# Windowed attention and a ternary feed-forward layer on one core: the attention stage written anew, with head tiles on TensorE and each even half of the keys kept twice

## What is computed

```python
xn = layernorm(x)
qkv = xn @ Wqkv + bqkv                       # 16 heads of 32 features
scores = q_block @ keys_of_3_blocks.T / sqrt(512)   # blocks of 128 tokens
scores = where(abs(kpos - qpos) <= 128 and 0 <= kpos < S, scores, -1e30)
attn = softmax(scores) @ values_of_3_blocks
a = attn @ Wout + bout
h = xn @ (scale * ternary(w_fc)).T + gate * (xn @ v.T @ fast_b.T @ u.T)
f = max(h, 0)**2 @ (scale * ternary(w_proj)).T
out = x + a + f
```

## Time and profile before

| | before |
|---|---|
| median of 3 runs | 2811.32 us |
| the profiled execution | 2808.96 us |
| its span, first to last instruction | 2807.0 us |
| mean granted TensorE clock | 0.984 |
| busy: TensorE, VectorE, ScalarE, GpSimd | 97%, 72%, 61%, 23% |
| instructions | 61651 |

### The profile page before, as it was taken

How to read it: one execution, slowest core, us unless ns; L and a number is a source line. 1 busy time by engine, 2 the same in 40 slices (tenths; PEclk the granted TensorE clock), 3 DMA queues, 4 the chain that set the end, 5 groups by cost and what they waited for, 6 DMA issues and landing times. The chain is left out here.

```text
span 2807.0 us, 61651 instructions
## 1 busy us (share of the span) xinstructions
PE 2728.3 (97%) x20744; PEld 2397.7 (85%) x20744; DVE 2023.4 (72%) x5704; ACT 1712.8 (61%) x3745; POOL 639.1 (23%) x812
## 2 busy tenths in 40 slices
PE   6999999999999999999999977999999999999998
PEld 5899999999999999999999965888888888888887
DVE  4899999999999999999999966444444444444443
ACT  3678778787787877878778756333333333333332
POOL 3223323233233332323323220111111111111111
PEclk9999999999999999999999987999999999999999
DMA  3333333333333333333333333111111111111101
GB/s 114 92 97 93 99 94 105 89 92 100 95 98 96 94 99 94 99 94 94 99 95 95 97 90 137 49 46 49 45 50 46 49 46 45 46 45 46 45 31 45
DMA packets 177015, 219.98 MB, mean 78 GB/s; under 512 B 32112, under 2 KB 115280, under 8 KB 176192
## 3 DMA queue, kind: packets, MB, share of 16 engines
q1 hardware_dynamic: 175840, 215.31, 26.7%
q0 software_dynamic: 864, 0.73, 0.1%
HBM read 80.91 MB, written 33.55 MB: 41 GB/s over the span
## 5 line engine op out<-in xcount | busy, mean ns | idle before, releaser
L716 ACT ACTIVATE probs<-neg_scores,neg_max 128x384 f32<-128x384 f32 (+1 forms) x1024 | 630.8, 616 | 341.9 <-DVE neg_max L789 335.3
L789 DVE CUSTOM_DVE_ANT_0 neg_scores<-score_ps,mask 128x384 f32<-128x384 f32 (+1 forms) x1024 | 559.9, 547 | 109.0 <-PE score_ps L913 56.2
L1441 ACT ACTIVATE relu<-up_ps,fc_scale 128x512 f32<-128x512 f32 x256 | 176.3, 689 | 656.9 <-PE up_ps L1572 656.9
L800 DVE TENSOR_TENSOR pT_lo<-pT_ps,pT_hi 128x384 f16<-128x384 f32 (+1 forms) x1024 | 561.2, 548 | 13.5 <-ACT xT_hi L729 4.9
L1515 DVE SCALAR_TENSOR_TENSOR sq<-up_ps,relu 128x512 f32<-128x512 f32 x256 | 177.0, 691 | 536.2 <-ACT relu L1441 536.2
L934 PE MATMUL pT_ps<-ident,probs 128*128 128x128 f32 x3040 | 506.6, 275 | 12.4 <-ACT probs L716 9.8
L727 ACT CAST pT_hi<-pT_ps 128x384 f16<-128x384 f32 (+1 forms) x1024 | 470.1, 459 | 3.8 <-PE pT_ps L934 3.5
L913 PE MATMUL score_ps<-stack 96*128 96x128 f32 (+2 forms) x1536 | 448.9, 347 | 0.0
L934 PEld LDWEIGHTS pT_ps<-ident,probs 128*128 128x128 f32 x3040 | 366.0, 141 | 81.3 <-DVE oT_lo L804 12.9
L1582 PE MATMUL down_ps<-proj_T,sq_hi 128*128 128x512 f32 x1024 | 408.9, 399 | 0.3 <-DVE sq_lo L1498 0.2
L1584 PE MATMUL down_ps<-proj_T,sq_lo 128*128 128x512 f32 x1024 | 404.3, 395 | 0.0
(11 more groups left out here) (165 smaller groups left out, 5186.1 us busy)
## 6 DMA issues: line engine op xcount, KB each, us to landing
stack<-qk_parts SPq DMA_DIRECT2D x1536, 64.0 KB, 2.1
x_in<-in_L_attn_x SPq DMA_DIRECT2D x64, 256.0 KB, 3.2
y<-in_L_attn_x SPq DMA_DIRECT2D x64, 256.0 KB, 3.0
partial<-y SPq DMA_DIRECT2D x64, 256.0 KB, 3.4
f_x_in<-in_L_attn_x SPq DMA_DIRECT2D x64, 256.0 KB, 2.7
part_in<-partial SPq DMA_DIRECT2D x64, 256.0 KB, 3.6
out<-f_y SPq DMA_DIRECT2D x64, 256.0 KB, 2.0
fc_in<-in_L_ffn_w_fc SPq DMA_DIRECT2D x16, 256.0 KB, 6.2
```

Of the source, the lines that this page charges most:

```text
L716: nc.scalar.activation(probs[:, r, cols], neg_scores[:, r, cols], ACT.Exp, bias=neg_max[:, s % 4:s % 4 + 1], scale=-1.0).then_inc(probs_do ...
L789: nc.vector.tensor_tensor_reduce(out=neg_scores[:, r, cols], in0=score_ps[:, r, cols], in1=mask[:, cols], scale=-SCORE_SCALE, scalar=3e38, ...
L800: last = nc.vector.tensor_tensor(pT_lo[:, s % 4, cols], pT_ps[:, r, cols], pT_hi[:, s % 4, cols], ALU.subtract)
```

## The change

The feed-forward stage now comes first. It is the same, but for three things: it adds x where it added `partial`, and writes x plus feed-forward to `partial`; it also stores the turned, normalised x, hi and lo, to a new DRAM tensor (8 DMAs of 256 KB per tile); and its 14 inner tiles are a hardware loop of 7 rounds of two tiles, with semaphore values in registers.

The attention stage (`attention_stage`) reads the turned x from DRAM, so its layernorm and transposes of x are gone. It has 128 steps of four heads by two query blocks (one step does what 8 steps did before). In a step t:

- `scores`: for each of the two blocks three passes (q_hi k_hi, q_lo k_hi, q_hi k_lo), each four matmuls, one for each head: 32 rows by 384 columns, at four places of the array (`tile_position=(h * DH, 0)`) and into four PSUM banks. The `stack` tile and its DMAs are gone.
- Keys are kept for six blocks; `copy_keys` on GpSimd copies the new even half to the front, so that 384 keys are always in one piece.
- The exponential also sums its row (`accum_out`), VectorE inverts the sums, GpSimd multiplies the probabilities in SBUF, TensorE turns them, and ScalarE alone copies them to an f32 tile `pT`; no f16 parts.
- `probs_times_values`: values are stationary (128 x 32, plain f32), the turned probabilities are moving, with four heads at four column places (`tile_position=(0, h * DH)`): per step 8 matmuls of 256 columns and 8 of 128. The product is already turned for the output projection.

The cut diff (of 1732 lines):

```diff
@@ feed-forward, loop over tiles
-            for i in range(NT):
-                tile(i, i % 2)
+            tile(0, 0)
+            with eng.Fori(0, (NT - 2) // 2) as pair:
+                for n in range(2):
+                    tile(2 * pair + 1 + n, (1 + n) % 2)
+            tile(NT - 1, (NT - 1) % 2)
@@ feed-forward, sync
+            def store_xT(i, par):
+                for b in range(NB):
+                    sp.wait_ge(xT_done, NB * i + b + 1)
+                    settle(sp, ticks)
+                    for low, xT in enumerate((xT_hi, xT_lo)):
+                        sp.dma_start(xT_rows(xT_dram, NB * i + b, low),
+                                     xT[:, par, :, b * P:(b + 1) * P].bitcast(F32)).then_inc(xT_stored[b], 16)
@@ attention, all of it replaced; GpSimd
+            def normalise(t, b):
+                ...
+                pool.wait_ge(rcp_done, 2 * t + b + 1)
+                for h in range(HC):
+                    u = b * HC + h
+                    nc.gpsimd.tensor_scalar(probs[:, u, cols], probs[:, u, cols], sum_rcp[:, u:u + 1], None, ALU.mult
+                                            ).then_inc(normalised, 1)
+            def copy_keys(u):
+                i, c = where(u)
+                pool.wait_ge(qk_done, u + 1)
+                nc.gpsimd.tensor_copy(k_hi[:, c, 0:2, :], k_hi[:, c, 4:6, :])
+                nc.gpsimd.tensor_copy(k_lo[:, c, 0:2, :], k_lo[:, c, 4:6, :]).then_inc(keys_copied, 1)
@@ ScalarE
+            def exp(t, b, h):
+                ...
+                nc.scalar.activation(probs[:, u, cols], probs[:, u, cols], ACT.Exp, bias=neg_max[:, u:u + 1], scale=-1.0,
+                                     accum_out=prob_sum[:, u:u + 1]).then_inc(exped, 1)
+            def copy_pT(t, b, h):
+                ...
+                act.wait_ge(turned, 8 * t + b * HC + h + 1)
+                if t >= 1:
+                    act.wait_ge(pv_done, t)
+                nc.scalar.copy(pT[:, h, first + seen.start:first + seen.stop, :].rearrange("p w t -> p (w t)"),
+                               pT_ps[:, h % 2, seen.start * P:seen.stop * P]).then_inc(pT_done, 1)
+            for t in range(STEPS + 3):
+                ...
+                for h in range(HC):
+                    if 1 <= t <= STEPS:
+                        copy_pT(t - 1, 1, h)
+                    if t < STEPS:
+                        exp(t, 0, h)
+                if job_a(t) is not None:
+                    qk_high(job_a(t), A_NUMBER[t], a_bank(t))
+                for h in range(HC):
+                    if t < STEPS:
+                        exp(t, 1, h)
+                    if h == 0 and 1 <= t <= STEPS:
+                        oT_high(t - 1)
+                    if t < STEPS:
+                        copy_pT(t, 0, h)
@@ VectorE
+                if t < STEPS:
+                    find_max(t, 0)
+                    invert_sums(t, 0)
+                if job_a(t) is not None:
+                    qk_low(job_a(t), a_bank(t))
+                if t < STEPS:
+                    find_max(t, 1)
+                if 1 <= t <= STEPS:
+                    oT_low(t - 1)
+                if t < STEPS:
+                    invert_sums(t, 1)
@@ TensorE
+                for pass_ in range(PASSES):
+                    q = q_lo if pass_ == 1 else q_hi
+                    keys = k_lo if pass_ == 2 else k_hi
+                    for h in range(HC):
+                        rows = slice(h * DH, (h + 1) * DH)
+                        last = nc.tensor.matmul(score_ps[:, h, cols], q[rows, c, place, :],
+                                                keys[rows, c, first + seen.start:first + seen.stop, :],
+                                                start=(pass_ == 0), stop=(pass_ == PASSES - 1),
+                                                tile_position=(h * DH, 0))
+                ...
+                for n, (blk, places, seen) in enumerate(parts):
+                    for h in range(HC):
+                        ...
+                        last = nc.tensor.matmul(job_ps[strip, bank, places.start * P:places.stop * P],
+                                                values[:, blk % VR, head * DH:(head + 1) * DH], pT[:, h, seen, :],
+                                                start=(n == 0), stop=(n == len(parts) - 1), tile_position=(0, h * DH))
+            for t in range(STEPS + 3):
+                if t < STEPS:
+                    scores(t, 0)
+                for part in range(QUARTERS):
+                    if 1 <= t <= STEPS:
+                        turn_probs(t - 1, 1, part)
+                    run_a(t, part)
+                if t < STEPS:
+                    scores(t, 1)
+                if 1 <= t <= STEPS:
+                    probs_times_values(t - 1)
+                for part in range(QUARTERS):
+                    if t < STEPS:
+                        turn_probs(t, 0, part)
+                    run_b(t, part)
```

More of the change, by code:

```diff
@@ L46, in settle, with xT_rows @@
     eng.sem_inc(ticks[eng.engine], 1)
+    eng.sem_inc(ticks[eng.engine], 1)
 def block_rows(dram, block):
     return dram[bass.ds(block * P, P), :]
+def xT_rows(dram, block, low):
+    return dram[bass.ds((2 * block + low) * P, P), :].rearrange("p (k t) -> p k t", k=DC)
 def identity_on_pool(pool, nc, ident, zeroed, ready):
@@ L1270, in _, with feed_forward_stage @@
                 nc.scalar.copy(low_out[:, n * D:(n + 1) * D], turn_ps[0:3 * DH, n, :]).then_inc(u_copied, 1)
-def feed_forward(nc, x, partial, fast_b, w_fc, w_proj, u, v, gate, out):
+def feed_forward_stage(nc, x, fast_b, w_fc, w_proj, u, v, gate, xT_dram, partial):
     F = w_fc.shape[0]
@@ L1334, in feed_forward @@
         stored = [sem(f"stored{b}") for b in range(NB)]
+        xT_stored = [sem(f"xT_stored{b}") for b in range(NB)]
         block = ctx.enter_context(nc.Block())
@@ L1367, in _ @@
                 sp.sem_inc(stored[b], 16)
+            def store_xT(i, par):
[5 more added lines that the diff above has]
+                                     xT[:, par, :, b * P:(b + 1) * P].bitcast(F32)).then_inc(xT_stored[b], 16)
+            store_xT(0, 0)
             def tile(i, par):
@@ L1375, in tile @@
                         settle(sp, ticks)
-                        sp.dma_start(block_rows(out, NB * (i - 1) + b), y[:, b, :]).then_inc(stored[b], 16)
+                        sp.dma_start(block_rows(partial, NB * (i - 1) + b), y[:, b, :]).then_inc(stored[b], 16)
                 for b in range(NB):
-                    sp.dma_start(part_in[:, b, :], block_rows(partial, NB * i + b)).then_inc(part_here[b], 16)
+                    sp.dma_start(part_in[:, b, :], block_rows(x, NB * i + b)).then_inc(part_here[b], 16)
+                if not is_last(i):
+                    store_xT(i + 1, 1 - par)
             tiles(sp, tile)
@@ L1382, in _ @@
                 sp.wait_ge(y_done, NB * (NT - 1) + b + 1)
-                sp.dma_start(block_rows(out, NB * (NT - 1) + b), y[:, b, :]).then_inc(stored[b], 16)
+                sp.dma_start(block_rows(partial, NB * (NT - 1) + b), y[:, b, :]).then_inc(stored[b], 16)
             for b in range(NB):
                 sp.wait_ge(stored[b], 16 * (NT + 1))
+                sp.wait_ge(xT_stored[b], 32 * NT)
         @block.gpsimd
@@ L1415, in xT_high @@
                 act.wait_ge(x_turned, NB * i + b + 1)
+                wait(act, xT_stored[b], 32 * (i - 1))
                 nc.scalar.copy(xT_hi[:, par, :, b * P:(b + 1) * P],
@@ L1610, with attention, feed_forward @@
+HELD = {}
+def attention(nc, x, Wqkv, bqkv, Wout, bout, partial):
+    HELD["attention"] = (Wqkv, bqkv, Wout, bout)
+def feed_forward(nc, x, partial, fast_b, w_fc, w_proj, u, v, gate, out):
+    xT_dram = nc.dram_tensor("xT", [2 * x.shape[0], x.shape[1]], F32, kind="Internal").ap()
+    feed_forward_stage(nc, x, fast_b, w_fc, w_proj, u, v, gate, xT_dram, partial)
+    attention_stage(nc, *HELD["attention"], xT_dram, partial, out)
 _INS = ["L0_attn_x", "L0_attn_Wqkv", "L0_attn_bqkv", "L0_attn_Wout", "L0_attn_bout", "L0_ffn_fast_b", "L0_ffn_w_fc",
```

1257 lines of the change are left out of this document (464 added, 793 removed).

## The result

The changed kernel takes 2876.74 us, the median of 4 runs (2875.95 to 2878.27), against 2811.33 us (2810.37 to 2813.68, 4 runs): the ratio is 1.0232, with a 95% interval of 1.0214 to 1.025. The forecast was 2765 us, faster; the time lies within its range of 2650 to 3000, but on the other side of no change. The profiled execution took 2878.27 us, with a span of 2875.8.

What follows compares the result with a forecast made beforehand. TensorE was taken to bound the kernel, at 12.09 us per attention step against 12.54. The span was 2807.0 - 128 x 0.45 + 14 = 2763, with 2 us around it 2765 us; range 2650 to 3000.

Steps and rivals of the forecast that it cites:

- The chain: Attention: cross-engine waits from turning probabilities to turning them a step later, 11.2 us; as rival it binds, 2651 us, 17%.
- Hidden by TensorE's work: Attention step: the 11.2 us of waits around the engines lie below TensorE's 12.09 us, so they cost nothing.
- TensorE's sum: Attention step: TensorE's own work adds up to 12.09 us, 0.45 less than the 12.54 of before.
- Values: TensorE's product of probabilities with values, plain f32: two heads at a time, 2.58 us a step.
- Scores: TensorE's 24 score matmuls of a step: six passes of four heads at 0.22 us, 1.32 us.
- Turns and changes of work: TensorE per step: 24 transposes 1.92 us, plus 0.6 for changes between kinds of work and short waits.
- Jobs: TensorE per step: the qk job 2.83 us and the v or out job 2.84, both unchanged.
- Loads in line: Rival, 16%: the four weight loads of a score pass follow each other, scores 2.64 us, step 13.4, 2934 us.
- An array that drains: Rival, 12%: TensorE's array empties at five changes of places a step, 1.25 us more, step 13.3, 2924 us.
- Places that don't run side by side: Rival, 15%: array places work one at a time, scores 4.27 us, values 5.16, step 17.6, 3430 us.
- None is the bound by sum: Attention step: ScalarE 8.9 us, VectorE 6.4 and GpSimd 5 to 9 of busy time, so none of them binds.
- The loop: Feed-forward stage: its 7 hardware loop rounds cost 2 us each, 14 us in all.

Runs made afterwards that it cites:

- the run with 0.52: Also called the run with 96 columns: on the changed kernel, GpSimd multiplies only the first 96 of 384 columns (0.52 us a product); 2715.18 us, ratio 0.9659.

## Why the prediction was wrong

**The step that failed** is "GpSimd: the multiplication of 384 columns has no row. ... 384 columns are 0.47 to 0.97, I take 0.5, for it has one input of that size." It measured 1.244 us, over both ends. The prediction itself had named a multiplication over 1.2 us as what would make it wrong. The two rows of GpSimd were a cast and an addition, and neither is a product with a scalar per row; of the two the one that I set aside, the two-input form, was the nearer. The bounds should have had room above the dearer row.

**A second error let it pass.** The chain had the product once, and the text concluded "if the multiplication is 0.97, it is 11.7, still below". With 1.24 in the same place it would have come to 11.9, still below 12.09. But turns go in fours, each with its own product, and beyond 1.03 us a head all four count: 0.72 + 3 x 0.19 = 1.29 us from the run with 0.52 to the changed kernel, measured 1.26.

**The rest of the chain** was 11.2 us and measured 11.78 with a product of 0.52. Laid beside the chain of waits of the run with 96 columns, the main shortfalls are the three heads ahead of the last (3 x 1.03, I had 3 x 0.95) and the four exponentials with their copies (3.9, I had 3.7). An exponential with its sum costs ScalarE 0.66 there (2006.81 - 2006.15; I had 0.60), and a turn lasts 0.53 until ScalarE sees it (I had 0.24 + 0.2). "Hidden by TensorE's work" fails by itself, since TensorE's sum is 11.45. By the run with 96 columns, a product of 0.52 makes it about 2715 us: had the product cost what I took, the kernel would have been faster, as forecast, but the chain would have set its time and not TensorE.

**TensorE's sum**, forecast 12.09, measured 11.45. Values 2.58 against 1.44: four places at a time, not two, so near the lower bound of 1.29. Against one at a time (5.16 and 4.27 us by the prediction's pitches) the column places give 3.6 times and the row places 2.9 times. Scores 1.32 against 1.45. Turns and changes of work 1.92 + 0.6 against 2.94. Jobs 5.67 against 5.62. The errors cancel in part and leave 0.64 us, and TensorE's sum did not set the step.

**The other rivals.** Loads in line: no, a pass of four heads starts 0.18 to 0.28 us after the last. An array that drains for 1.25 us a step: no; what the turns take above 24 x 0.08 us is 1.02 us a step, of which I had 0.6 already. Behind scores or values a turn takes 0.48 us in place of 0.33, so something is paid at a change, but not the price weighed there. Places that don't run side by side: no (its time was also added up wrongly: its step of 17.6 gives about 3475 us, not 3430). The chain: it binds, as that rival says, but at 13.04 us, and the sign came out the other way. The chance of 0.46 for slower rested on mechanisms that did not occur, and that the time lies within the stated range is luck: nothing that the range was made of gives it.

**Off the path.** "None is the bound by sum" holds: from 1800 to 2400 us ScalarE is busy 9.6 us a step (forecast 8.9), VectorE 5.8 (6.4), GpSimd 10.8 (5 to 9), all under 13.04. The loop: 14 us forecast, measured none that shows. Start and end of the stage: 70.6 kept, 74 measured.

## What to carry to other kernels

Price an instruction by a row of its own form on its own engine; where there is none, keep the bound open above the dearest neighbour, and ask first what the kernel costs if the price doubles. When one engine prepares pieces that the next takes one by one, compare its time per piece with the pace of the taker: below it only the first counts, above it each does. Before a piece of work goes to a faster engine, read what stands behind it in that engine's list: VectorE's product is three times as fast as GpSimd's and gained about 12 us, where a cheaper form on GpSimd gained 123.

## What the runs showed of the hardware that I had not expected

- In these runs GpSimd multiplies 384 columns by a scalar per row in 1244 ns (923 at 256, 763 at 192, 523 at 96), and in 827 ns with two inputs, the second with a stride of 0.
- When VectorE and GpSimd multiply at the same time, both slow: 417 to 581 ns and 1244 to 1354.
- Four column places in plain f32 work side by side only when neighbours in the list use different places: 1.44 against 4.10 us for the same 32 passes.
- Four row places in float32r work side by side in either order: 2671.6 against 2676.4 us, with first passes that start 3 or 10 ns apart. Why the two kinds differ is open; the types differ too.
